# First of two sorts of a graph's edges: the counts of all blocks ahead of the ranks, and the first 140 columns placed 14 at a time

## The reference

```python
xn = _layernorm(x, axis=-1)
messages = xn[dst] * edge_weight[:, None]
agg = jax.ops.segment_sum(messages, src, num_segments=6250)
h = relu((xn + agg) @ W1 + b1) @ W2 + b2                    # L0_gnn
x = x + h + _L0_mix(xn)                                     # linear attention
x = x + _L0_ffn(_layernorm(x))
...                                                         # layer 1: agg1 = zeros.at[dst].add(xn1[src]), attention, experts
```

## Time and profile before

| | us |
|---|---|
| median of three timed runs | 6405.18 |
| lowest and highest | 6404.75, 6407.28 |
| span of the profiled execution | 7249.7 |
| VectorE, first sort | 7 to 251 |
| first scatter, last scatter of the first sort | 172, 1240 |
| A0 and B0 | 261 to 1445, 1445 to 2011 |
| first gather of the GNN stage | 2043 |

### The profile page before, as it was taken

One profiled execution on the slowest core, in us unless ns is written; L12 is line 12 of the kernel. 1 busy time (PEld: TensorE's weight loads), 2 busy tenths in 40 slices (PEclk: granted clock), 3 DMA queues, 4 the chain that ended last, 5 costly groups with the idle time before them and its releaser, 6 DMA issues.

```text
span 7249.7 us, 87859 instructions
## 1 busy us (share of the span) xinstructions
PE 5328.2 (73%) x24977; PEld 4445.0 (61%) x24977; DVE 3382.5 (47%) x9891; ACT 1308.8 (18%) x2962; POOL 3860.9 (53%) x4349
## 2 busy tenths in 40 slices
PE   0111110667659999999899999979999899997794
PEld 0000000556537777777678887868788778876682
DVE  8511100666645555555464464436444554446323
ACT  0000000111101111111142242214111231111240
POOL 0777776000055555555888888830666326654205
PEclk9755555778779999999999999989999999999895
DMA  1000000221133333335310011021333223353223
GB/s 37 9 12 12 12 12 11 73 66 58 59 105 98 96 99 100 98 97 93 49 48 18 14 40 34 20 70 48 91 95 97 76 71 107 108 93 109 89 94 117
DMA packets 319771, 477.56 MB, mean 66 GB/s; under 512 B 99008, under 2 KB 240054, under 8 KB 319470
## 3 DMA queue, kind: packets, MB, share of 16 engines
q0 software_dynamic: 153136, 262.81, 14.8%
q1 hardware_dynamic: 166334, 211.17, 9.5%
HBM read 371.27 MB, written 102.33 MB: 65 GB/s over the span
## 4 chain that ended last, share of the span: by engine, by line
PE 57%; another core or an unknown queue 13%; DVE 11%; issue 11%; DMA 4%; DVEq 2%; ACT 1%; SPq 1%; POOL 1%; ACTq 0%; POOLq 0%
PE bank L2277 13%; PE bank L2288 13%; PE bank L2505 5%; PE bank L2338 5%; PE bank L2487 4%; PE bank L2323 4%; PE bank L2774 3%; PE bank L2630 2%; PE bank L2268 2%; PE bank L2816 1%; DMA sb_work_QT<-scratch_q 1%; DMA sb_rows<-scratch_xn,sb_row_of 1%; DMA sb_work_XC<-in_x 1%; DVE sb_STATE L1391 1%
## 5 line engine op out<-in xcount | busy, mean ns | idle before, releaser
L995 POOL DMA_INDIRECT sb_rows<-scratch_xn,sb_row_of x1760 | 1718.7, 977 | 1553.2 <-PE bank L2323 619.1
L988 POOL DMA_INDIRECT scratch_sorted<-sb_FREE x1564 | 1589.6, 1016 | 546.5 <-issue 379.2
L2288 PE MATMUL bank<-sb_work_FT,sb_W 128*128 128x250 f32 x4400 | 1006.9, 380 | 19.6 <-ACT sb_work_FT L1075 15.1
L2288 PEld LDWEIGHTS bank<-sb_work_FT,sb_W 128*128 128x128 f32 x4400 | 845.3, 193 | 134.6 <-ACT sb_work_FT L1075 22.0
L1075 ACT ACTIVATE sb_HT<-bank,sb_cols 128x250 f32<-128x250 f32 x1333 | 552.8, 467 | 2047.2 <-PE bank L2487 811.6
L2277 PE MATMUL bank<-sb_W,sb_HT 128*125 128x256 f32 x4000 | 894.2, 380 | 1.1 <-ACT sb_HT L1075 1.1
L2277 PEld LDWEIGHTS bank<-sb_W,sb_HT 128*125 128x125 f32 x4000 | 752.7, 188 | 115.4 <-ACT sb_HT L1075 1.9
L2277 PE MATMUL bank<-sb_W,sb_work_FT 128*125 128x256 f32 x1600 | 409.3, 406 | 449.8 <-issue 378.3
L2277 PEld LDWEIGHTS bank<-sb_W,sb_work_FT 128*125 128x125 f32 x1600 | 315.0, 201 | 518.0 <-issue 450.5
L2323 PE MATMUL bank<-sb_rows,sb_work_TM 128*125 128x257 f32 x1760 | 444.8, 392 | 91.2 <-issue 29.7
L1660 DVE TENSOR_TENSOR sb_FREE<-sb_FREE,bank 125x257 f32 x440 | 186.1, 423 | 698.0 <-PE bank L2323 455.1
(11 more groups left out here) (375 smaller groups left out, 7606.2 us busy)
## 6 DMA issues: line engine op xcount, KB each, us to landing
sb_rows<-scratch_xn,sb_row_of POOLq DMA_INDIRECT x1760
scratch_sorted<-sb_FREE POOLq DMA_INDIRECT x1564
scratch_qT<-sb_work_QF SPq DMA_DIRECT2D x100, 250.0 KB
sb_work_QF<-scratch_qT SPq DMA_DIRECT2D x100, 250.0 KB
sb_work_XC<-in_x SPq DMA_DIRECT2D x50, 250.0 KB
sb_work_ZT<-scratch_xn SPq DMA_DIRECT2D x50, 250.0 KB
sb_W<-in_L_mix_W SPq DMA_DIRECT2D x9, 1024.0 KB
sb_work_XC<-scratch_zs SPq DMA_DIRECT2D x28, 256.0 KB, 2.6
```

Source lines behind the costliest of these rows:

```text
L988: nc.gpsimd.indirect_dma_start(out=sorted_d[e], out_offset=bass.IndirectOffsetOnAxis(ap=pos[e][0:n, c:c + 1], axis=0), in_=rec[e][0:n, 2 * ...
L995: nc.gpsimd.indirect_dma_start(out=rows[:, t % RING, 0:D], out_offset=None, in_=table, in_offset=bass.IndirectOffsetOnAxis(ap=row_of[:, t: ...
L2288: ins = nc.tensor.matmul(dst[:, b, :], w[:, k0 + k, 128 * (b0 + b):128 * (b0 + b) + 128], source[:, k, :], start=(n == 0), stop=(n == 2 * ...
```

## The change

VectorE's first sort is rewritten; the second sort stays as it is, apart from names.
- The totals of the 25 pairs of blocks come from one operation each, the one-hot with its sum as a second output; nothing is scanned and no rank is made here. The counts are unpacked and the groups worked out as before. The casts and field writes that stood ahead of the ranks now follow the unpacking of the counts.
- Ten strips of 14 columns each are placed for all 50 blocks at once. A strip is a tile of 50 rows of 15 numbers per partition: the first number of a row is where the block's next edge goes (`base` − 1, later the last sum of the strip before), the other 14 are one-hots. One scan over all 750 numbers (a mask `strip_keep` of ones, with zeros at the row starts, makes the rows independent) gives each edge its place; a product with the one-hots and a reduce over the blocks pick it out, and five small operations turn it into a row of the table. GpSimd waits per strip.
- For the other 642 columns each block takes a compare, a scan that begins at the block's place, and a predicated copy into `start`; the 50 blocks are unrolled, in three stages of a pipeline, with four buffers for the compares and two for the scans.

```diff
-FIRST_COLUMNS = 96
+STRIP = 14
+STRIPS = 10
+FIRST_COLUMNS = STRIP * STRIPS
...
             def scatter(e, c):
-                for n, chunk in enumerate(CHUNKS[e]):
-                    if c == chunk.start:
-                        pool.wait_ge(sort_step, placed(e, n + 1))
-                        hold(pool)
+                if columns_placed(e, c):
+                    pool.wait_ge(sort_step, columns_placed(e, c))
+                    hold(pool)
...
+            nc.vector.memset(strip_keep, 1.0).then_inc(strip_kept, 1)
+            dve.wait_ge(strip_kept, 1)
+            nc.vector.memset(strip_keep[:, :, 0:1], 0.0).then_inc(strip_kept, 1)
             dve.wait_ge(edges_loaded, 96)
...
+            def sort_first_counts():
...
+                for k in range(NT // 2):
+                    dve.wait_ge(sort_step, FIRST_READY - NT // 2 + max(k - 1, 0))
+                    nc.vector.scalar_tensor_tensor((is_b, scan)[k % 2], half, iota_b[:, k:k + 1], step_of,
+                                                   ALU.is_equal, ALU.mult, accum_out=packed[:, k:k + 1])\
+                        .then_inc(sort_step, 1)
+                dve.wait_ge(sort_step, FIRST_READY)
+                step = steps(FIRST_READY)
+                decode_counts(step)
+                step(nc.vector.tensor_copy(scan, dst_i))
+                step(nc.vector.scalar_tensor_tensor(f0, scan, 128.0, f0, ALU.mult, ALU.add))
+                step(nc.vector.tensor_copy(f1, ew))
+                step(nc.vector.memset(tmp, 0.0))
...
+            def slots_placed(step, e, columns):
+                at, slot = (x[:, columns] for x in (start, lane))
+                step(nc.vector.tensor_scalar(slot, at, 63.5, 1.0 / 128, ALU.subtract, ALU.mult))
+                step(nc.vector.tensor_scalar(slot, slot, ROUND, ROUND, ALU.add, ALU.subtract))
+                step(nc.vector.scalar_tensor_tensor(at, slot, -128.0, at, ALU.mult, ALU.add))
+                step(nc.vector.scalar_tensor_tensor(at, at, float(NS), slot, ALU.mult, ALU.add))
+                step(nc.vector.tensor_copy(pos[e][:, columns], at))
+
+            def sort_first_strips():
+                dve.wait_ge(strip_kept, 2)
+                step = steps(FIRST_BASED)
+                own = strip_is[:, :, 1:STRIP + 1]
+                lanes = iota_b[:].rearrange("p (b u) -> p b u", u=1).to_broadcast([P, NT, STRIP])
+                for n in range(STRIPS):
+                    columns = slice(STRIP * n, STRIP * (n + 1))
+                    if n:
+                        step(nc.vector.tensor_copy(strip_is[:, :, 0], strip_sums[:, :, STRIP]))
+                    else:
+                        step(nc.vector.tensor_scalar(strip_is[:, :, 0], base, -1.0, None, ALU.add))
+                    step(nc.vector.tensor_tensor(own, blk[:, columns].rearrange("p (u c) -> p u c", u=1)
+                                                 .to_broadcast([P, NT, STRIP]), lanes, ALU.is_equal))
+                    step(nc.vector.tensor_tensor_scan(strip_sums.rearrange("p b c -> p (b c)"),
+                                                      strip_keep.rearrange("p b c -> p (b c)"),
+                                                      strip_is.rearrange("p b c -> p (b c)"), 0.0, ALU.mult, ALU.add))
+                    step(nc.vector.tensor_tensor(strip_own, own, strip_sums[:, :, 1:STRIP + 1], ALU.mult))
+                    step(nc.vector.tensor_reduce(start[:, columns], strip_own.rearrange("p b c -> p c b"), AX.X, ALU.add))
+                    slots_placed(step, 0, columns)
+
+            def sort_first_rest():
...
+                for b in range(NT + 2):
+                    if b < NT:
+                        after(("copy", b - 4))
+                        mark(nc.vector.tensor_scalar(masks[b % 4], blk[:, columns], iota_b[:, b:b + 1], None, ALU.is_equal),
+                             "is", b)
+                    if 0 <= b - 1 < NT:
+                        after(("is", b - 1), ("copy", b - 3))
+                        mark(nc.vector.tensor_tensor_scan(counts[(b - 1) % 2], masks[(b - 1) % 4], tmp[:, columns],
+                                                          strip_sums[:, b - 1, STRIP:STRIP + 1], ALU.add, ALU.add),
+                             "scan", b - 1)
+                    if 0 <= b - 2:
+                        after(("scan", b - 2), ("copy", b - 3))
+                        mark(nc.vector.copy_predicated(start[:, columns], masks[(b - 2) % 4].bitcast(I32),
+                                                       counts[(b - 2) % 2]), "copy", b - 2)
+                dve.wait_ge(sort_step, FIRST_PLACED - 5)
+                slots_placed(steps(FIRST_PLACED - 5), 0, columns)
...
             dve.wait_ge(consts_made, 8)
-            sort_prepare(0)
-            with dve.Fori(0, NT // 2) as k:
-                sort_rank(0, k)
-            sort_decode(0)
+            sort_first_counts()
             sort_groups(0)
-            for n in range(len(CHUNKS[0])):
-                with dve.Fori(0, NT // 2) as k:
-                    sort_start(0, n, k)
-                sort_place(0, n)
+            sort_first_strips()
+            sort_first_rest()
             sort_blocks(0)
-            sort_prepare(1)
+            sort_prepare_second()
```

More of the change, by code:

```diff
@@ L54 @@
 PADDING = 1 << 24
+HIGH = (SECOND / 2 - 0.5, 1.0 / SECOND)
 RING = 8
@@ L801, in load_l1 @@
                                   ((wk, "k"), (wv, "v"), (wq, "q"), (wo, "o"))])
-            sp.wait_ge(sort_step, placed(0, len(CHUNKS[0])) + BLOCKS[0])
+            sp.wait_ge(sort_step, PLACED_AT[0] + BLOCKS[0])
             def blocks_of(j):
@@ L1355, in steps, with fields_of, blocks_of_keys @@
                 return step
-            def sort_prepare(e):
-                key, other = ((src_i, dst_i), (dst_i, src_i))[e]
+            def fields_of(e):
                 fields = rec[e].rearrange("p (c f) -> p c f", f=2)
-                def field(n):
-                    return fields[:, :, n:n + 1].rearrange("p c u -> p (c u)")
-                step = steps(SORT_BASE[e])
+                return [fields[:, :, n:n + 1].rearrange("p c u -> p (c u)") for n in range(2)]
+            def blocks_of_keys(step, key):
                 step(nc.vector.tensor_copy(keyf, key))
@@ L1374, in sort_prepare, with sort_prepare_second @@
                 step(nc.vector.tensor_scalar(step_of, odd, SECOND - 1.0, 1.0, ALU.mult, ALU.add))
[L1375 to L1380, removed]
+            def sort_prepare_second():
+                f0, f1 = fields_of(1)
+                step = steps(SORT_BASE[1])
+                blocks_of_keys(step, dst_i)
+                step(nc.vector.scalar_tensor_tensor(f0, blk, float(-T), keyf, ALU.mult, ALU.add))
+                halves_of_blocks(step)
+                step(nc.vector.tensor_copy(scan, src_i))
+                step(nc.vector.scalar_tensor_tensor(f0, scan, 128.0, f0, ALU.mult, ALU.add))
+                step(nc.vector.memset(f1, 1.0))
@@ new lines, in sort_first_rest, with after, mark @@
+            def sort_first_rest():
+                columns = slice(FIRST_COLUMNS, EC)
+                masks = [x[:, columns] for x in (is_b, rank, keyf)]
+                masks.append(strip_is.rearrange("p b c -> p (b c)")[:, 0:EC - FIRST_COLUMNS])
+                counts = [x[:, columns] for x in (scan, lane)]
+                done = {}
+                def after(*marks):
+                    dve.wait_ge(sort_step, max([FIRST_REST] + [done[x] for x in marks if x in done]))
+                def mark(ins, *of):
+                    ins.then_inc(sort_step, 1)
+                    done[of] = FIRST_REST + len(done) + 1
+                for b in range(NT + 2):
[14 more added lines that the diff above has]
+                slots_placed(steps(FIRST_PLACED - 5), 0, columns)
@@ L1400, in sort_decode @@
                 step = steps(SORT_BASE[e] + RANKED)
[L1401 to L1409, removed]
+                decode_counts(step)
+                step(nc.vector.tensor_scalar(is_b, rank, *HIGH, ALU.subtract, ALU.mult))
                 step(nc.vector.tensor_scalar(is_b, is_b, ROUND, ROUND, ALU.add, ALU.subtract))
@@ L1418, in sort_groups @@
                 dve.wait_ge(sort_sums, 3 * e + 1)
-                step = steps(SORT_BASE[e] + DECODED)
+                step = steps(DECODED_AT[e])
                 step(nc.vector.memset(start, 0.0))
@@ L1445, in sort_start, with sort_place_second @@
                     dve.wait_ge(sort_step, k * 4 + (before + 2 * j + 1))
-                    nc.vector.tensor_tensor(start[:, cols], start[:, cols], buffer[:, cols], ALU.add)\
+                    nc.vector.tensor_tensor(start, start, buffer, ALU.add)\
                         .then_inc(sort_step, 1)
-            def sort_place(e, n):
-                begun = placed(e, n) + 2 * NT
+            def sort_place_second():
+                begun = SORT_BASE[1] + BASED + 2 * NT
                 dve.wait_ge(sort_step, begun)
                 step = steps(begun)
[L1453 to L1460, removed]
```

(4 more changed lines are left out.)

62 lines of the change are left out of this document (48 added, 14 removed).

## The result

| | before | after |
|---|---|---|
| median of the timed runs, us | 6406.01 (4 runs) | 6298.16 (4 runs, 6297.91 to 6299.74) |
| ratio | 1 | 0.9832, 95% interval 0.9818 to 0.9846 |
| span of the profiled execution, us | 7249.7 | 6295.7 |
| time of that execution, us | not known | 6297.91 |

The change gains 108 us, 1.7%.

The account below looks back on a forecast made before the run. Two chains, VectorE's sorts with A0 and B0 and GpSimd's 782 scatters, meet at the first gather, the scatters later by 24 us. Gaining that 24 and losing VectorE's 12: 6405.2 − 24 + 12 = 6393 us, range 6358 to 6424.

Parts of the forecast that it names:

- The frame: A0's 854.8 us stall is the trace's own; without it 6394.9 us, 5206.8 following the GNN stage's first gather.
- main chain: VectorE's first sort, second-sort preparation, A0, B0, end of second sort; first gather at 1188, after the change 1200.
- A scatter beside A0 and B0 at 1.34 us: GpSimd's first-sort scatters: 1.34 us each with VectorE about 65% busy, between 1.265 and 1.38; last one at 1222.
- The lead of the scatter chain: At the first gather: GpSimd's scatters and the record load end later than VectorE's path by 10 to 45, taken as 24.
- VectorE 12 us later: First sort: 235 us added, 223 removed, so A0 starts 12 us later (0 to 24).
- Scatters 104 us earlier: GpSimd, first sort: first scatter at 56 instead of 171.88 us, last at 1118 instead of 1222.
- After the change the main chain ends last, with 70 us to spare: At the first gather after the change: VectorE's path at 1200, the scatters' path at 1129.
- Rival 1: VectorE's path already ends last in timed runs; only its 12 us count: 6417 (6405 to 6429), chance 0.26.
- Rival 2: First sort's strips or rest dearer than the rows, VectorE 30 us later: 6411 (6400 to 6425), chance 0.12.
- Rival 3: The A0 stall is in timed runs too; fewer scatters beside it save 91 less 12: 6326, chance 0.06.

Follow-up runs that it names:

- again: The kernel before, unchanged, profiled once more: 6402.21 us in one execution, span 6400.4.
- eight: The changed kernel with eight scatters in flight instead of four: 6278.87 us, ratio 0.9801.
- idle20: The changed kernel with twenty more VectorE memsets between the first sort and A0: 6305.31 us, ratio to before 0.9842.
- eight_idle20: The changed kernel with eight scatters in flight and twenty more VectorE memsets ahead of A0: 6300.73 us, ratio 0.9841.

## Why the prediction was wrong, step by step

**The frame.** "The timed run is only 10.3 us over that" was true and meant nothing: two errors cancelled. The step that all hung on was that what follows the first gather is 5206.8 us for both. It is 5081.5: the disturbed execution was stretched there too, by 125.3 us, without a stall as plain as the one in A0 (29 us up to the second sort's records, 80 from there to the last gather, 17 behind it). And the first gather without the stall was not at 1188 but at 1318.9, 130.9 us later. 1188 was right for the main chain alone: VectorE is done at 1184.53 in again, and in eight the first gather comes 4.8 us behind that point. 130.9 − 125.3 = 5.6, and with the 1.8 us around the span of again, and the 3.0 from its time to the median 6405.18, the sum is 10.4, the 10.3 seen. A total that agrees is evidence for a sum only if each part has been looked at; I looked for the stretch in one stage and took the rest as sound.

**A scatter beside A0 and B0 at 1.34 us.** This is the term that failed. In again it was (597.6 + 241.3)/559 = 1.50 us from 262 to 1100. GpSimd's own part was 1.38, the upper end of the range and not 1.34: 20 us of the 86 by which the last scatter of before came later than forecast (1308 instead of 1222). The larger part, 0.12 us a scatter or 70 us, is the landing wait, which the sum put at nothing. (The end of the queue, 1.32 us a scatter behind 1100, gives 4 us back.) It could not be seen in the trace of before, because there the stall had thinned the very transfers that the scatters wait beside: in rows 2 the stretch 261 to 1202 runs at 11 GB/s with 691 scatters in 941 us, while A0 without stall runs at 78. The row for 172 to 245, which I used for a busy VectorE, has 1 GB/s. So both ends of my range, 1.265 and 1.38, came from stretches with few transfers, and the 68 GB/s of the third line of rows 2, in a stretch without scatters, was the warning. The rows bounded VectorE's influence and left the DMA traffic out.

In after one sees it directly. GpSimd, and SyncE's stores of the same pair (lines of one stretch, 290 to 305 us):

```profile
293.40 5.18 SPq L766 DMA_DIRECT2D scratch_xn<-sb_work_ZT  x2
298.87 2.65 SPq L770 DMA_DIRECT2D scratch_xT<-sb_work_FT  x2
```

```profile
294.48 1.45 POOL L1013 DMA_INDIRECT scratch_sorted<-sb_FREE  x1 [0.30 <-issue]
298.37 0.95 POOL L1013 DMA_INDIRECT scratch_sorted<-sb_FREE  x1 [2.44 <-DMA scratch_sorted<-sb_FREE]
300.14 0.95 POOL L1013 DMA_INDIRECT scratch_sorted<-sb_FREE  x1 [0.82 <-DMA scratch_sorted<-sb_FREE]
```

The waits stand where the x loads and the stores of a pair are issued, once per pair. From 53 to 245 us, at 1 GB/s, there is next to no landing wait even with two in flight: one, of 0.8 us. That the stage's transfers are the cause is read from this, and was not tested by taking them away.

**The lead of the scatter chain.** By my own rows it was 45 us; I took 24, because the total of the frame spoke for 10. It was 130.5, VectorE's wait in again. With the frame left out I would have been less wrong.

**VectorE 12 us later.** It was 0.6. Counts: 24.0 us (14.01 to 37.99) instead of 28. Each is an operation of 1027 ns, and neighbours start 0.955 us apart, the 80 ns read of the sum among it; the overlap that I granted to the rest was left out here. The Trainium skill, "VectorE: DVE Perf Modes", section "Two Vector instructions with no wait between them", says that such an operation is two instructions; the trace agrees, and prices the second at 80 ns, hidden by the overlap. Strips: 62.8 (46.47 to 109.23) instead of 61. The reduce that strides by 14 took 1340 ns, where a straight operation on 700 elements takes 887: the upper bound of its price (0.87 + 0.45) was the right one. Rest: 133.6 (109.23 to 242.83) instead of 143: the scan took 1.54 us and not 1.47, but the three steps of a block recur every 2.66 us, where their durations add up to 2.90. Sum of the three errors −4 + 2 − 9 = −11, which is the difference.

**Scatters 104 us earlier.** Right: 102.6 (1308.32 to 1205.74), though both ends were nearly 90 us off. First scatter at 53.3 (forecast 56). The error per scatter is in both kernels and cancels in the difference, which is why it can't be noticed there.

**After the change the main chain ends last, with 70 us to spare.** Wrong: the scatter chain ends last by 27.7 us. So no part of the 104 us was lost to the other chain, where the forecast let through only 24 less 12.

**The rivals.** Rival 1 (main chain already last) is refuted by the 130.46 us wait in again. Rival 2 did not happen, VectorE being 0.6 us later, and would have cost next to nothing: its 30 us stand against 27.7 us of slack, and idle20 moves the first gather by 0.8 us with 19 of them. Rival 3 gave 6326, the number nearest to the result, for a wrong reason: no stall is in the timed runs and A0 is not relieved. Missing from my list was the simplest rival: the scatter chain is later than I think by more than the change moves it, all 104 us count, 6301. I had both numbers for it, and the sentence "if the median falls by more than 60 us: then scatters cost A0 time" shows that I saw only the other reading.

## What to carry to other kernels

When a profiled execution is longer than the timed ones, don't repair it by taking out the one stall that can be seen: profile again first, and if that can't be had, take no price for a resource from a stretch in which the stall has emptied it. For a queue of small transfers, price the work of the issuing engine and the wait for landing apart; the latter depends on how many may fly and on what else is moving, and raising the number in flight was worth 66 us in the kernel before for one changed number. Two chains that meet are told apart by delaying one on purpose: 19 us on VectorE moved the first gather by 0.8 us in after and by 18.1 in the version with eight in flight.

## What the runs showed of the hardware that I had not expected

- One profiled execution of a kernel was 13% longer than its timed runs (7249.7 us against 6405.18). Against a second one its first gather came 724.0 us later (854.8 us of stall in A0, less the 130.9 by which the scatters are late in any case), and what follows took 125.3 us longer. The second one of the same kernel was not stretched (6400.4), nor were the eight of the other kernels. What brought it about stays open.
- Scatters of 128 records, 8 bytes each, land up to 8.8 us after their issue beside the transfers of A0 and B0 and within 3.3 us at 1 GB/s; two in flight take 2.21 us each at 78 GB/s, four 1.54 and eight 1.37, while GpSimd's own part is 1.38 to 1.44. That the transfers are the cause was not tested by taking them away.
- Three operations of VectorE on 782 columns took 1.45, 2.13 and 2.54 us instead of 0.57, 0.57 and 0.97 while GpSimd ran a memset and two selects over 32x2048 (runs eight and eight_idle20). The scatters themselves show no slowing of its predicated copy: 835 ns for the 642 columns of the rest beside them, where 1022 × 642/782 is 839.
- Beside a DMA rate of 1 GB/s two in flight are enough: from 53 to 245 us two and four in flight have 135 and 136 scatters, with 0.8 us and nothing of landing wait.
